# An attention loop regrouped from one batch at a time to rounds of one head pair and both batches

## The reference

```
h = gelu(x[:, 1:] @ W1 + x[:, :1] @ W2 + b)                  # 16 x 255 rows
z = layernorm(h); q, k, v = z @ Wq.T, z @ Wk.T, z @ Wv.T     # 16 heads of 64
h = h + softmax(q @ k.T / 8) @ v @ Wo.T + bo
z = layernorm(h)
probs = softmax(z @ router_w); the 2 best of 8 experts per row, with their probabilities
routed = sum over those experts of prob * (silu(z @ w1[e]) @ w2[e])
shared = sigmoid(z @ gate_w) * ((silu(z @ gate) * (z @ up)) @ down)
h = h + routed + shared
```

## Time and profile before

| | us |
|---|---|
| median of three runs | 1110.76 (1110.05 to 1113.36) |
| the profiled execution, own time | 1112.86 |
| its span, first to last instruction | 1111.1 |
| TensorE busy | 1051.8 (95%) |
| VectorE busy | 757.1 (68%) |
| ScalarE busy | 673.6 (61%) |
| GpSimd busy | 512.6 (46%) |
| mean granted TensorE clock | 0.987 of full speed |

### The profile page before, as it was taken

The page is one execution under the profiler, slowest core; times in us unless marked ns, Lnnn a source line. Parts: engine busy times, 40 slices in busy tenths (PEclk is TensorE's granted clock), DMA queues, the critical chain, the costliest instruction groups (busy, mean ns, idle before and its releaser), DMA issues.

```text
span 1111.1 us, 23557 instructions
## 1 busy us (share of the span) xinstructions
PE 1051.8 (95%) x8042; PEld 880.7 (79%) x8042; DVE 757.1 (68%) x1975; ACT 673.6 (61%) x2067; POOL 512.6 (46%) x557
## 2 busy tenths in 40 slices
PE   6979999999999999999999999999997979999996
PEld 5867778878787887887788778878775869998985
DVE  3756775786778577667857766775775656666667
ACT  4647774775677477567747756774775545554531
POOL 0024543546446364645546464554435376444430
PEclk9989999999999999999999999999999989999999
DMA  8110000001000000100000010000003733444369
GB/s 265 59 44 1 1 1 20 2 1 40 19 1 23 19 20 1 40 20 1 21 21 21 1 40 20 1 11 30 21 1 105 252 101 103 134 133 133 123 215 309
DMA packets 47498, 65.93 MB, mean 59 GB/s; under 512 B 7992, under 2 KB 39480, under 8 KB 47384
## 3 DMA queue, kind: packets, MB, share of 16 engines
q1 hardware_dynamic: 40056, 44.50, 12.8%
q0 software_dynamic: 7056, 19.93, 5.3%
q10 hardware_dynamic: 272, 0.00, 0.0%
HBM read 36.09 MB, written 28.33 MB: 58 GB/s over the span
## 4 chain that ended last, share of the span: by engine, by line
PE 70%; POOL 7%; DVE 6%; issue 6%; DMA 3%; ACT 2%; SPq 1%; another core or an unknown queue 0%; DVEq 0%; POOLq 0%; ACTq 0%
PE pT_ps L714 10%; PE o_ps L727 9%; PE proj_ps L69 9%; PE proj_ps L71 9%; PE proj_ps L70 8%; PE s_ps L700 8%; POOL prob L1655 2%; PE v_ps L69 2%; PE v_ps L70 2%; PE v_ps L71 2%; POOL prob L1657 2%; PE s_ps L69 2%; DMA back<-expert_out_rows 2%; PE s_ps L70 2%; PE s_ps L71 2%
## 5 line engine op out<-in xcount | busy, mean ns | idle before, releaser
L1015 ACT ACTIVATE prob<-s_ps,nmax 128x255 f32<-128x255 f32 x512 | 238.7, 477 | 228.1 <-DVE nmax L1222 228.0
L1655 POOL TENSOR_SCALAR prob<-prob,rinv 128x255 f32<-128x255 f32 x128 | 139.4, 1089 | 375.0 <-DVE rinv L1240 370.6
L1222 DVE TENSOR_REDUCE nmax<-s_ps 128x2 f32<-128x510 f32 x256 | 166.3, 682 | 37.8 <-PE s_ps L700 36.3
L714 PEld LDWEIGHTS pT_ps<-ident,prob 128*128 128x128 f32 x1024 | 109.6, 141 | 60.7 <-issue 49.8
L714 PE MATMUL pT_ps<-ident,prob 128*128 128x128 f32 x1024 | 146.0, 281 | 6.7 <-POOL prob L1657 3.5
L1247 DVE COPY probT<-pT_ps 128x512 f32<-128x512 f32 x128 | 88.5, 691 | 76.9 <-PE pT_ps L714 76.9
L727 PE MATMUL o_ps<-probT,v 128*64 128x256 f32 x1024 | 139.6, 394 | 1.2 <-DVE oT_lo L1253 1.2
L700 PE MATMUL s_ps<-qk_space 64*128 64x256 f32 x1536 | 125.4, 296 | 5.3 <-ACT prob L1015 4.6
L1657 POOL TENSOR_SCALAR prob<-prob,rinv 128x255 f32<-128x255 f32 x128 | 118.9, 929 | 0.0
L700 PEld LDWEIGHTS s_ps<-qk_space 64*128 64x128 f32 x1536 | 99.2, 185 | 21.9 <-issue 8.7
L1015 ACT ACTIVATION_READ_ACCUMULATOR prob<-s_ps,nmax 128x1 f32 x512 | 106.5, 208 | 0.0
(11 more groups left out here) (265 smaller groups left out, 2717.8 us busy)
## 6 DMA issues: line engine op xcount, KB each, us to landing
xg<-expert_in_rows SPq DMA_DIRECT2D x71, 130.0 KB
back<-expert_out_rows SPq DMA_DIRECT2D x6, 1024.0 KB, 21.2
xin<-in_x_dram SPq DMA_DIRECT2D x8, 512.0 KB, 4.6
z_rows<-z SPq DMA_DIRECT2D x8, 512.0 KB, 3.2
z<-z_rows SPq DMA_DIRECT2D x8, 512.0 KB, 5.8
expert_in_rows<-bo_row SPq DMA_DIRECT2D x16, 128.0 KB
raw_up<-in_L_ffn_w_dram SPq DMA_DIRECT2D x8, 256.0 KB, 4.8
raw_down<-in_L_ffn_w_dram SPq DMA_DIRECT2D x8, 256.0 KB, 6.2
```

Source lines behind the costliest of these rows:

```text
L714: m = pe.transpose(pT_ps[h][:, o:o + P], prob[u_par(i)][:, h, qt, kt * P:(kt + 1) * P], ident[:])
L1015: m = act.activation(prob[u_par(i)][:, h, qt, 1:N], s_ps[h][:, qt * N + 1:(qt + 1) * N], ACT.Exp, bias=nmax[u_par(i)][:, n:n + 1], accum_o ...
L1222: dve.tensor_reduce(nmax[u_par(i)][:, 2 * h:2 * h + 2], s_ps[h][:].rearrange("p (q k) -> p q k", q=2)[:, :, 1:N], AX_X, ALU.max, negate=Tr ...
L1655: pool.tensor_scalar(prob[k][:, 0, 1, 1:N], prob[k][:, 0, 1, 1:N], rinv[k][:, 1:2], None, ALU.mult).then_inc(s_nA1, 1)
```

## The change

The unit of work becomes a round: one head pair w (counted through all groups, 64 in all) and both batches b. On TensorE a round is, in order: the scores of pair w+1 for both batches; the products of pair w-1 for both; the transposes of pair w, batch 0; Q of pair w+2; the transposes of pair w, batch 1; K of pair w+2; the work for the group before, if any (`between`); two tiles of V. The numbers of matmuls stay as they were.

The banks are shared out anew: four for scores (one per batch and head), two for transposed probabilities, one (`proj_ps`) for Q and then V, one (`o_ps`) for the products and then K. So K waits until the product before it has been read (`s_ol`), V until Q has been read, and the next product until K has been read. Products and V leave their banks in one instruction of 512 columns where there were two of 256. There are four probability buffers where there were two, and the routing's transposed rows lie over a part of `oT_hi` and `oT_lo`.

The 96 matmuls by Wo of a group stand together in round 0 of the next, in score banks. The routing's steps are attached to rounds: VectorE's row statistics to round 1, normalised rows to 1, transposed rows to 2, logits to 3, probabilities, best two and one-hot to 4, ranks to 5, places and slots to 6. The last round puts matmuls by Wo between its waits. The load of experts 4 to 7 also waits for the last logits.

```diff
-        s_ps = [bank(f"s_ps{h}") for h in range(2)]
+        s_ps = [[bank(f"s_ps{b}{h}") for h in range(2)] for b in range(2)]
         pT_ps = [bank(f"pT_ps{h}") for h in range(2)]
         o_ps = bank("o_ps")
-        proj_ps = [bank(f"proj_ps{j}") for j in range(2)]
-        v_ps = bank("v_ps")
+        proj_ps = bank("proj_ps")
+        qk_ps = (proj_ps, o_ps)
...
+            def project_qk(w, n):
+
+                g, p = w // PAIRS, w % PAIRS
+                hi, lo = ((wq_hi, wq_lo), (wk_hi, wk_lo))[n]
+                cols = slice(p * P, (p + 1) * P)
+                if n == 0:
+                    if w:
+                        pe.wait_ge(s_ve, w)
+                elif w < AHEAD + 1:
+                    if w:
+                        pe.wait_ge(s_qkl, 2 * w)
+                else:
+                    pe.wait_ge(s_ol, w - AHEAD)
...
+            def project_v(w):
+                p = w % PAIRS
+                pe.wait_ge(s_qkl, 2 * w + 1)
...
+            def scores(w, b):
+                u = 2 * w + b
+                (q_hi, q_lo), (k_hi, k_lo) = qk[w % 2]
+                pe.wait_ge(s_qkl, 2 * w + 2)
+                if w:
+                    pe.wait_ge(s_exp, 2 * (u - 2) + 2)
...
+            def round_of(g, r):
+                w = PAIRS * g + r
+                scores(w + 1, 0)
+                if g and r:
+                    between_read(g, r - 1)
+                scores(w + 1, 1)
+                if w:
+                    values(w - 1)
+                transpose_p(w, 0)
+                if w + AHEAD < LAST:
+                    project_qk(w + AHEAD, 0)
+                transpose_p(w, 1)
+                if w + AHEAD < LAST:
+                    project_qk(w + AHEAD, 1)
+                if g:
+                    between(g, r)
+                if w + AHEAD < LAST:
+                    project_v(w + AHEAD)
+                if r == LAST_OLD and g + 1 < GROUPS:
+                    for c in range(DC):
+                        transpose_z(g + 1, c)
...
         @block.scalar
...
+            def round_of(g, r):
+                w = PAIRS * g + r
+                exps(w + 1, 0, 0)
+                exps(w + 1, 0, 1)
+                exps(w + 1, 1, 0)
+                probT_a(w, 0)
+                if w:
+                    o_hi(w - 1)
+                exps(w + 1, 1, 1)
+                if w + AHEAD < LAST:
+                    qk_hi(w + AHEAD, 0)
+                normalise_b1(w + 1, 0)
+                if g and r == 4:
+                    router_exps(g - 1)
+                probT_a(w, 1)
+                if w + AHEAD < LAST:
+                    qk_hi(w + AHEAD, 1)
+                normalise_b1(w + 1, 1)
+                if g and r == 2:
+                    for c in range(DC):
+                        z2_hi(g - 1, c)
+                if w + AHEAD < LAST:
+                    v_copy(w + AHEAD)
+                if r == LAST_OLD and g + 1 < GROUPS:
+                    for c in range(DC):
+                        z_hi(g + 1, c)
...
         @block.vector
...
+            def round_of(g, r):
+                w, q = PAIRS * g + r, g - 1
+                maxima(w + 1, 0, 0)
+                maxima(w + 1, 0, 1)
+                maxima(w + 1, 1, 0)
+                maxima(w + 1, 1, 1)
+                if g and r == 1:
+                    row_stats(q, 0)
+                    row_stats(q, 1)
+                normalise_a(w + 1, 0)
+                probT_b(w, 0)
+                if w:
+                    o_lo(w - 1)
+                if g and r == 4:
+                    probabilities(q)
+                elif g and r == 6:
+                    places(q)
+                normalise_a(w + 1, 1)
+                if w + AHEAD < LAST:
+                    qk_lo(w + AHEAD, 0)
+                probT_b(w, 1)
+                if g and r == 4:
+                    best_two(q)
+                if w + AHEAD < LAST:
+                    qk_lo(w + AHEAD, 1)
...
```

More of the change, by code:

```diff
@@ L729, in values, with output_part @@
                 m.then_inc(s_o, 1)
-            def output_tile(t):
+            def output_part(t, ps, pairs):
                 rows = slice(t * P, (t + 1) * P)
-                for pair in range(PAIRS):
-                    m = three(pe, proj_ps[t // 2][:, (t % 2) * D:(t % 2 + 1) * D], oT_hi[:, pair, rows],
-                              oT_lo[:, pair, rows], wo_hi[:, pair, :], wo_lo[:, pair, :],
+                for pair in pairs:
+                    m = three(pe, ps, oT_hi[:, pair, rows], oT_lo[:, pair, rows], wo_hi[:, pair, :], wo_lo[:, pair, :],
@@ new lines, in router_ranks, with between @@
+            def router_ranks(q, ps):
+                pe.wait_ge(s_taken, q + 1)
+                pe.matmul(ps[:, 0:GT * E], before[:], taken[:].rearrange("p t e -> p (t e)"), start=True, stop=True)
+                pe.matmul(ps[:, GT * E:2 * GT * E], ones[:], taken[:].rearrange("p t e -> p (t e)"),
+                          start=True, stop=True).then_inc(s_rank, 1)
+            def between(g, r):
+                q, R = g - 1, PAIRS * g + r
+                exps_done = min(2 * (2 * (R + 1) + 1) + 1, 4 * LAST)
+                if r == 0:
+                    pe.wait_ge(s_ol, PAIRS * g)
+                    for j in range(2):
+                        pe.wait_ge(s_exp, exps_done + j)
+                        output_rows(q, j)
+                elif r == 2:
+                    pe.wait_ge(s_z2, GT * q + GT)
+                    for c in range(DC):
+                        pe.wait_ge(s_exp, exps_done + c)
+                        transpose_z2(q, c)
+                elif r == 3:
+                    pe.wait_ge(s_exp, exps_done)
+                    router_logits(q)
+                elif r == 5:
+                    pe.wait_ge(s_exp, exps_done)
+                    router_ranks(q, rows_ps[0])
@@ L1136, in _ @@
             hidden_split_hi(0, 0)
-            router_step(GROUPS, 3)
-            router_step(GROUPS, 4)
+            for c in range(DC):
+                z2_hi(GROUPS - 1, c)
             z3_hi(1)
@@ L1481, in _ @@
                 z_lo(0, c)
-            for j in range(4):
-                qk_lo(0, j)
-                if j == 1:
-                    maxima(0, 0, 0)
-                    maxima(0, 0, 1)
-                    normalise_a(0, 0)
+            qk_lo(0, 0)
+            qk_lo(0, 1)
+            for b in range(2):
+                for h in range(2):
+                    maxima(0, b, h)
+            qk_lo(1, 0)
+            normalise_a(0, 0)
+            qk_lo(1, 1)
+            normalise_a(0, 1)
             dve.wait_ge(s_r, 1)
```

727 lines of the change are left out of this document (336 added, 391 removed).

## The result

| | before | changed | forecast |
|---|---|---|---|
| median of 20 runs each, us | 1111.2 (1108.6 to 1114.7) | 1123.6 (1110.9 to 1130.1) | 1098.5 (1079 to 1114) |
| profiled execution / its span, us | 1112.9 / 1111.1 | 1117.6 / 1115.9 | 1100.6 |
| mean granted TensorE clock | 0.987 | 0.978 | |

The ratio to the kernel before is 1.0069, 95% interval 1.0043 to 1.0094: 0.7% slower, little but clear of the noise, where I forecast 1.1% faster. The ratio leaves out five runs of the changed kernel that lie over 1.5% above its fastest; the median of the other fifteen is 1117.6 us. Among these fifteen the time grows as the mean clock of the run falls: 1110.9 us at 0.984, 1117.6 at 0.978, 1124.0 at 0.974, 1125.9 at 0.970.

The account below looks back on a forecast made before the run. The prediction took TensorE, busy for 95% of the span, as the bound. Its terms, -30.7 - 18.0 + 42.4 - 6 = -12.3 us, gave 1100.6 for the profiled execution and 1098.5 for the median, range 1079 to 1114 (its own 1086 to 1108).

Parts of the forecast that it names:

- Shape changes: TensorE's switches between full, half-row and half-column matmuls: 64 sets go at 0.48 us each, saving 30.7 us.
- Old waits: TensorE's waits in the groups of the kernel before: they go with the old order, saving 18.0 us.
- new waits: TensorE waiting in rounds for VectorE's steps: 6.2 us a group, 42.4 us in all, largest 2.71 in round 4.
- The walk: Step-by-step timing of VectorE and ScalarE through the rounds: plain round 9.68 us, new waits 42.4 us in all.
- Tail: Run's end up to the shared layer's first matmul: matmuls by Wo between its waits save 6 us, bounds 0 and 9.2.
- rival B: TensorE's clock halves behind waits of rounds 4 to 6, once per group: 12 us, so 1111 us; chance 0.10.
- the wait of the earlier trace: TensorE's 1.1 us idle before zT's low part, kernel before: clock kept 1.00 through it, cited against rival B.
- the sum's own bounds: Low and high ends of terms: shape changes save 18 to 31 us, new waits cost 5 to 63, tail saves 0 to 9.2.
- A: VectorE's steps fit between its waits in the rounds: new waits only 21 us, so 1077 us; chance 0.13.
- C: Chain of the product's bank, shared with K, lengthens each round by some 0.3 us: 20 us, 1119 us; chance 0.15.

Follow-up runs that it names:

- c1: The changed kernel, unaltered, on another chip: 1099.0 us, ratio 0.9954 to the kernel before.
- e6: Changed kernel plus one 64-column matmul between V's two tiles: full array in round 1, half rows in 2, half columns in 3; single run, 1095.7 us.
- c2: The changed kernel, unaltered, on another set's chip: 1122.6 us, ratio 1.0084 to the kernel before.
- c3: The changed kernel, unaltered, on the last set's chip: single run, 1120.2 us (kernel before there 1114.5).
- e1: Changed kernel with a group's fourth pair of indirect DMAs moved between the next round 0's two normalisations, never over two in a row: 1107.5 us, ratio 0.9951.
- e12: Changed kernel plus one GpSimd addition of 256 columns between the second and third pairs of indirect DMAs: single run, 1106.2 us.
- e7: Changed kernel with indirect DMAs spread, statistics beside the matmuls by Wo, exponentials early, VectorE's blocks one a round, group 0's constants later: 1061.5 us, ratio 0.9603.
- e10: e7 with probabilities behind K's low part, one-hot in round 6, ranks in 7, places and slots in the next round 0: 1066.2 us, ratio 0.9581.
- e13: Kernel before with all eight indirect DMAs of a group in a row behind the group's last normalisation: single run, 1143.2 us.
- e2: Changed kernel plus 16 small useless matmuls ahead of V in round 4 of groups 1 to 7: 1114.0 us, ratio 1.0010.
- e8: Same kernel as e2, run again beside the unaltered changed kernel on one chip: 1113.9 us, ratio 1.0019.

## Why the prediction was wrong

*Shape changes, -30.7.* The size is right: a plain round takes 9.68 us, and group 3 of c1 has the forecast period. In the round at 101.32 the scores take 1.63 us (twice 0.91 before), the products 1.88 (twice 1.02), and the second transposes 0.79 (0.85), near the forecast's places. What each change costs by its shape is shown for one only: by e6 a visit to half the rows from the full array costs 0.32. The product is entered from the half rows of the scores, which no run isolates, so why a set of products loses 0.15 is open. The Trainium skill (TensorEngine Tiling, Key Properties) has every change of tiling mode drain the engine; the half-row rows agree with it, the half-column row (0.34 as the full array) does not show it.

*Old waits, -18, new waits, +42.4.* Right in kind and nearly in size. Rounds 1, 2, 3: 10.21, 11.26, 11.39, as walked. Round 4 12.72 (the last group's 12.24) for 12.31, round 6 10.94 for 11.12, round 7 10.24 for 10.10. The walk along VectorE's and ScalarE's orders was good to 0.1 to 0.4 us a round.

*Tail, -6.* The stretch above is 1.8 us longer than forecast, beside the late round 0, so of the 6 us some 4 came. Not tested.

*The step that failed*, first half, is the one that let the sum stand at the full clock and gave rival B 0.10: "the same trace keeps 1.00 through the wait of the earlier trace rows". That was a wait of 1.12 us; my own walk had 2.25 for V in round 4, and 1.90 came. The same trace of before had the counterexample, in group 0, which I did not weigh (a row of TensorE's timeline, then a window):

```profile
85.53 1.36 PE L700 MATMUL s_ps<-qk_space 64*128 64x256 f32 x12 [2.73 <-ACT prob L1015]
...
86.00:89.30 3.30, 3.30 (x21) 1.94 (x18) 2.08 (x4) 2.50 (x9) 3.15 (x4) 0.50 0.00 0
```

One wait of 2.73 us, and half clock behind it, outside the tail. B's mechanism came true: 20.4 us of half clock in the profiled run. It cost 6.6 us, the growth of rounds 5, and not the 10 that its half would be, because part of it lies in round 4, where TensorE waits anyway. B's price of 12 us was high for this run; rounds 5 of c2 and c3 lost 8.5 and 9.2 us in groups 1 to 6. The Trainium skill (TensorE: Matmul & The Clock Gate, A second HAM failure mode), which I cited and set aside, describes short idle times between groups of matmuls that make the clock oscillate; the trace agrees that short idle times can, though here one wait of 1.90 us in a round stood ahead of each fall.

*Second half: a term that the sum does not have*, and no rival either. GpSimd's indirect DMAs change places with the rounds, and the prediction says nothing of them. Before, the pairs started 4.7 to 5.5 us apart (250.4, 255.9, 260.6, 265.6); in rounds, two of them stand back to back, 4.4 us behind a third, and TensorE's signals come late. Price: 1.4 to 1.5 us in six rounds, 8.5 us. Four of the five sets show it (the first comparison's, e1's, c2's, c3's); c1's does not, and there the change pays. That the place of these DMAs makes the difference is shown by e1 and e12; by which rule, and through what, is not.

*The range* was narrower than the sum's own bounds: shape changes at 18 instead of 30.7 alone give 1111.2, above the 1108 of the forecast's own range, and with new waits at 63 it would be 1131.8.

*Rivals A and C.* A: no, the forecast waits are all there. C: no, round 0 of c1, e1 and plain rounds show no wait of K for `oT_lo`, and a plain round is 9.68.

So of +17.1 us against the forecast in the profiled run, 8.5 are late signals, 6.6 the clock, 2.4 round 4; the rest nearly cancels. How the runs with a lower mean clock divide is not shown, as they have no trace.

## What to carry to other kernels

Merging two bodies of a loop saves at the seams and doubles the distance between the places where a helper engine has time; price each of its blocks by what stands behind it (here 1.06 us of probabilities ahead of K's low part cost round 4 0.74 us in e7, and behind it nothing in e10). Count a wait of TensorE as a risk for its clock with a price per run, not only as idle time, and look for the longest wait of the same trace that kept the clock and the shortest that lost it; filling it with useless matmuls shows at once whether the clock is the loss. Where GpSimd issues indirect DMAs, keep their spacing when you regroup work, and run on more than one chip before believing a difference under 1%.

## What the runs showed of the hardware

- TensorE's completion signals can come late though its matmuls keep pace: by 1 to 2 us with four indirect DMAs of GpSimd in a row 4.4 us behind a pair at the start of round 0, by 3.5 to 4.9 with eight in a row (e13, the copies against 1.13 us), not at all there with pairs 3.1 us or more apart; 0.7 us of other GpSimd work inside the four removed it (e12). In the middle of round 0 four in a row 4.2 us behind a pair made none later than 0.4 us (e10). One of the chips showed none of it. Through which part of the chip it comes stays open.
- The kernel before took 1104.4 us on one chip and 1111 to 1114.5 on the others.
- A matmul of 64 columns over half the rows between full ones costs 0.32 us more than one over the full array, over half the columns 0.00 (e6).
- Behind a single wait of 1.90 us the clock fell from 2.4 to 1.2 GHz in three to five of seven groups, for 3.4 or 6.8 us, and not at all in the others of the same runs, nor in any group of e6. It kept 2.4 GHz through a wait of 1.12 us and fell behind one of 2.73. With the 1.90 us filled by small matmuls it fell in one of fourteen rounds 4 (e2, e8).
